# Weighted sum of gathered expert rows: from scalar-tensor steps on VectorE to diagonal matmuls on TensorE, with a new order of all engines in the last stage

## The reference

```python
gathered = ye[e_flat, jnp.minimum(pos, CAP - 1)]
gathered = jnp.where(valid[:, None], gathered, 0.0) * topk_w.reshape(-1)[:, None]
routed = gathered.reshape(T, K, D).sum(axis=1).reshape(B, S, D)
...
scores = jnp.einsum('bsd,bmd->bsm', hidden_states, memory_tokens) * scale
scores = jnp.where(memory_mask[:, None, :], scores, neg_inf)
attn = jax.nn.softmax(scores, axis=-1)
readout = jnp.einsum('bsm,bmd->bsd', attn, memory_tokens)
```

## Time and profile before

| | us |
|---|---|
| median of 3 runs | 396.79 (394.83 to 396.96) |
| the profiled execution, its own time | 392.95 |
| its span (first to last instruction of the program) | 391.1 |
| busy in the span: PE / DVE / ACT / POOL | 291.7 / 289.8 / 222.2 / 183.9 |
| first gather of the last stage is issued at | 205.62 |
| last instruction on DVE starts at | 387.47 |

### The profile page before, as it was taken

One profiled execution on the slowest core, in us unless ns is written; L12 is line 12 of the kernel. 1 busy time (PEld: TensorE's weight loads), 2 busy tenths in 40 slices (PEclk: granted clock), 3 DMA queues, 4 the chain that ended last, 5 costly groups with the idle time before them and its releaser, 6 DMA issues. The chain is left out here.

```text
span 391.1 us, 6082 instructions
## 1 busy us (share of the span) xinstructions
PE 291.7 (75%) x1748; PEld 221.5 (57%) x1748; DVE 289.8 (74%) x916; ACT 222.2 (57%) x394; POOL 183.9 (47%) x310
## 2 busy tenths in 40 slices
PE   1699899789999988966999055775757577576755
PEld 1488788667788866855988033343434334253433
DVE  1782359999989892854850656779999999999971
ACT  1112345444654455533635136566889797999883
POOL 3430133343342116777307777878786866323000
PEclk9999999999999999999999655575596988999898
DMA  7999200000008107689635232221211222000011
GB/s 193 363 422 426 99 28 28 28 28 28 28 0 338 40 6 223 154 137 158 215 134 188 81 100 63 80 69 42 80 45 63 77 69 71 3 28 28 14 41 56
DMA packets 22802, 41.80 MB, mean 107 GB/s; under 512 B 3631, under 2 KB 18417, under 8 KB 22129
## 3 DMA queue, kind: packets, MB, share of 16 engines
q1 hardware_dynamic: 15920, 26.72, 18.6%
q0 software_dynamic: 4672, 12.59, 13.8%
q10 hardware_dynamic: 2176, 2.10, 1.7%
HBM read 33.01 MB, written 8.39 MB: 106 GB/s over the span
## 5 line engine op out<-in xcount | busy, mean ns | idle before, releaser
L545 POOL DMA_INDIRECT big<-ye_dram,dst_all x64 | 69.0, 1079 | 35.9 <-issue 19.5
L751 PE MATMUL psum<-q_w,rh 128*128 128x512 bf16 x128 | 40.9, 457 | 11.9 <-DVE upT L1345 7.3
L1284 DVE SCALAR_TENSOR_TENSOR x_all<-big,wk_all,x_all 128x256 f32<-128x256 f32 x64 | 31.0, 484 | 19.7 <-DMA big<-ye_dram,dst_all 18.0
L526 POOL DMA_INDIRECT big<-xn_dram,tix x32 | 32.3, 1009 | 13.8 <-issue 7.5
L479 POOL TENSOR_SCALAR ve<-mv 128x2 f32<-128x2 f32 x16 | 7.8, 489 | 53.3 <-DVE mv L1046 43.3
L751 PE MATMUL psum<-ctx_all,shup 128*128 128x256 f32 x128 | 29.5, 383 | 0.0
L751 PEld LDWEIGHTS psum<-q_w,rh 128*128 128x128 bf16 x128 | 13.0, 112 | 28.2 <-issue 19.1
L572 ACT ACTIVATE xnT<-psum 128x512 f32<-128x512 f32 x24 | 14.3, 596 | 24.1 <-PE psum L899 21.2
L751 PEld LDWEIGHTS psum<-ctx_all,shup 128*128 128x128 f32 x128 | 23.7, 190 | 3.0
L572 ACT ACTIVATE big<-psum 128x512 f32<-128x512 f32 x16 | 9.5, 596 | 27.5 <-PE psum L775 17.8
L942 PE MATMUL psum<-ident,xn 128*128 128x128 f32 x32 | 7.1, 360 | 23.0 <-ACT xn L597 23.0
(11 more groups left out here) (198 smaller groups left out, 831.8 us busy)
## 6 DMA issues: line engine op xcount, KB each, us to landing
upT<-in_upT_dram SPq DMA_DIRECT2D x1, 4096.0 KB, 16.5
dnT<-in_dnT_dram SPq DMA_DIRECT2D x1, 4096.0 KB, 26.0
ye_dram<-rh SPq DMA_DIRECT2D x16, 256.0 KB, 3.0
ctxT_all<-in_ctxT_dram ACTq DMA_DIRECT2D x8, 256.0 KB, 8.7
x_all<-in_x_dram SPq DMA_DIRECT2D x8, 256.0 KB, 9.0
xn_dram<-xn SPq DMA_DIRECT2D x8, 256.0 KB, 2.1
out_dram<-x_all SPq DMA_DIRECT2D x8, 256.0 KB, 2.2
ctx_all<-in_ctx_dram SPq DMA_DIRECT2D x1, 1536.0 KB, 7.7
```

What stands on the lines that cost most here:

```text
L526: pl.indirect_dma_start(out=xe[:, q, e, :], out_offset=None, in_=xn_dram[:, :], in_offset=bass.IndirectOffsetOnAxis(ap=tix[:, 2 * i.c + e: ...
L545: pl.indirect_dma_start(out=gath[:, s, t * TOPK + k, :], out_offset=None, in_=ye_dram[:, :], in_offset=bass.IndirectOffsetOnAxis(ap=dst_al ...
L751: return pe.matmul(o, l, r, start=first, stop=last, skip_group_check=True)
L1284: c(dve.scalar_tensor_tensor(xt(i, t), gath[:, s, t * TOPK + k, :], w, xt(i, t), ALU.mult, ALU.add))
```

## The change

The four multiply-adds per tile on DVE are replaced. DVE now builds, per tile, four 128 x 128 matrices with the weights on the diagonal (`weight_diag`, one tensor-tensor of 128 x 512 values, into the free half of `big`). PE multiplies them with the four gathered tiles and adds up in bank 5 (`rows_sum`, four matmuls of 128 x 256 in float32). DVE adds the sum to x (`combine`, one instruction) and takes the statistics (`row_stats`). Bank 5 is shared with the scores, so `rows_sum` also waits for `exps`, and `score` for `combine`. The softmax scale of 1/16 goes into the mask constants and into `copy_x2T`, and the negated maximum comes from the reduction itself, so one small instruction of `smax` is dropped. The lists of all four engines are in another order and with other lags.

```diff
+        diag = big[:, 1, 0:4 * TOPK * P].rearrange("p (s t k m) -> p s t k m", s=2, t=2, k=TOPK)
...
-            pl.memset(mscale[:, :], -NEG)
-            pl.memset(mneg1[:, :], NEG)
+            pl.memset(mscale[:, :], -NEG * SM_SCALE)
+            pl.memset(mneg1[:, :], NEG * SM_SCALE)
...
                 def stage(i, s):
-                    hold(pl, (c4[t], 6 * (i.c - 2) + 4))
+                    hold(pl, (cmb[t], i.c - 1))
                     for k in range(2 * part, 2 * part + 2):
                         pl.indirect_dma_start(
...
-                (1, rows(0, 1)), (2, x2_rstd), (1, rows(1, 0)),
-                (3, rstd_shift(x34, lambda i: i.at(8, 8), mvx, vex, rsx, shx, LN_EPS, rs5)), (5, h_rstd),
-                (1, rows(1, 1)), (0, rows(0, 0))])
+                (2, x2_rstd), (3, rstd_shift(x34, lambda i: i.at(8, 8), mvx, vex, rsx, shx, LN_EPS, rs5)),
+                (1, rows(1, 1)), (5, h_rstd), (1, rows(1, 0)), (0, rows(0, 1)), (0, rows(0, 0))])
...
-                copy_to(xnT[:, s, :, :], bank(4, K, 2 * P), xT4)
+                copy_to(xnT[:, s, :, :], bank(4, K, 2 * P), xT4, scale=SM_SCALE)
...
+            def rows_sum(t):
+
+                def stage(i, s):
+                    before = (c4[0], 3 * i.c + 1) if t else (c4[1], 3 * i.c - 2)
+                    hold(pe, (gin[s][t], 16 * TOPK * (i.c // 2 + 1)), (dgs[t], i.c + 1), (ex4, i.c if t else i.c - 1), before)
+                    for k in range(TOPK):
+                        ins = mm_(bank(5)[:, 0:D], diag[:, s, t, k, :], gath[:, s, t * TOPK + k, :],
+                                  k == 0, k == TOPK - 1)
+                    ins.then_inc(cmb[t], 1)
+                return stage
...
-                hold(pe, (xT4, i.c + 1), (ex4, i.c))
+                hold(pe, (xT4, i.c + 1), (ex4, i.c), (c4[0], 3 * min(i.c + 1, NP - 1) + 1), (c4[1], 3 * i.c + 1))
...
+            def weight_diag(t):
+
+                def stage(i, s):
+                    hold(dve, (cmb[t], i.c - 1), (rb, RB * NP), (wqs, 3 * NG))
+                    dve.tensor_tensor(diag[:, s, t, :, :], ident[:, None, :].to_broadcast([P, TOPK, P]),
+                                      wk_all[:, 2 * i.c + t, :, None].to_broadcast([P, TOPK, P]), ALU.mult)\
+                       .then_inc(dgs[t], 1)
+                return stage
+
             def combine(t):
 
                 def stage(i, s):
-                    c = Chain(c4[t], i, 6)
-                    hold(dve, (gin[s][t], 16 * TOPK * (i.c // 2 + 1)))
-                    for k in range(TOPK):
...
+                    hold(dve, (cmb[t], i.c + 1))
+                    dve.tensor_tensor(xt(i, t), bank(5)[:, 0:D], xt(i, t), ALU.add).then_inc(c4[t], 1)
+                return stage
+
+            def row_stats(t):
+
+                def stage(i, s):
+                    hold(dve, (c4[t], 3 * i.c + 1))
+                    dve.bn_stats(bn[:, s, t, :], xt(i, t)).then_inc(c4[t], 1)
+                    hold(dve, (c4[t], 3 * i.c + 2))
+                    dve.bn_aggr(mv[:, s, t, :], bn[:, s, t, :]).then_inc(c4[t], 1)
                 return stage
...
-                dve.tensor_reduce(smx[:, s, :], bank(5)[:, 0:2 * P].rearrange("p (t m) -> p t m", t=2), AX.X, ALU.max)\
-                   .then_inc(mx4, 1)
-                hold(dve, (mx4, i.at(2, 1)))
-                dve.tensor_scalar(nmx[:, s, :], smx[:, s, :], -SM_SCALE, None, ALU.mult).then_inc(mx4, 1)
+                dve.tensor_reduce(nmx[:, s, :], bank(5)[:, 0:2 * P].rearrange("p (t m) -> p t m", t=2), AX.X, ALU.max,
+                                  negate=True).then_inc(mx4, 1)
...
-                (0, late_shared), (2, x3), (4, h_(1)), (4, hw_(1)), (0, combine(0)), (3, h_(0)), (6, final(1)), (1, smax), (4, hscale),
-                (5, final(0)), (2, x3_absmax), (2, x_scale), (2, x3_quant), (0, combine(1)), (3, hw_(0))])
+                (6, hscale), (0, weight_diag(0)), (2, row_stats(0)), (7, final(0)), (5, h_(1)), (5, hw_(0)),
+                (2, combine(1)), (2, row_stats(1)), (3, x3), (0, weight_diag(1)), (4, h_(0)), (1, combine(0)),
+                (5, hw_(1)), (3, x3_absmax), (3, x_scale), (2, smax), (3, x3_quant), (7, final(1)), (1, late_shared)])
```

More of the change, by code:

```diff
@@ L315, in build @@
         c4 = [sem(f"combined{t}") for t in range(2)]
+        dgs, cmb = [sem(f"weight_diag{t}") for t in range(2)], [sem(f"rows_summed{t}") for t in range(2)]
         rs4, xn4 = sem("x2_rstd"), sem("x2_normed")
@@ L957, in pt @@
             def pt(i, s):
-                hold(pe, (ex4, i.c + 1), (xT4, i.c + 1))
+                hold(pe, (ex4, i.c + 1), (xT4, i.c + 1), (qT5, i.c))
                 for t in range(2):
@@ L1015, in _ @@
             run_steps(pe, NP, [
-                (4, hqt(0)), (3, project(1, 1, (hd[0], 1))), (2, project(0, 0, (sl[1], 0))), (4, hqt(1)), (0, x2t),
-                (2, project(1, 0, (hd[1], 0))), (5, down(1, (sl[0], 4))), (4, hqt(2)), (0, score),
-                (4, down(0, (sl[0], 3))), (4, hqt(3)), (0, pt),
-                (2, project(0, 1, (sl[0], 1), (fo[0], -1), (fo[1], -2))), (0, read), (1, xqt)])
+                (1, rows_sum(1)), (2, read), (5, hqt(0)), (3, project(1, 0, (hd[1], 0))),
+                (3, project(0, 1, (sl[0], 1))), (0, rows_sum(0)), (1, x2t), (5, hqt(1)),
+                (3, project(1, 1, (hd[0], 1))), (1, score), (6, down(1, (sl[1], 4))), (5, hqt(2)),
+                (5, down(0, (sl[1], 3))), (2, xqt), (5, hqt(3)), (1, pt),
+                (2, project(0, 0, (sl[1], 0), (fo[0], -2), (fo[1], -3)))])
         @block.vector
```

31 lines of the change are left out of this document (10 added, 21 removed).

## The result

In the timing the changed kernel has a median of 392.8 us over 20 runs, the kernel before 394.84 us over 20. The ratio is 0.994 with a 95% interval of [0.9914, 0.9966]: 0.6% faster, where 1.0% was forecast. The profiled execution took 391.8 us, its span is 390.1 us with a granted clock of 0.949, 1.0 us less than the span of before.

The account below looks back on a forecast made before the run. VectorE bounds the steady turn, busy 17.61 of 18.4 us. Turns -4.4, ramp +4.0, drain -3.7 sum to -4.1 us, so 396.79 becomes 392.7 us, 1.0% faster; range 386 to 402.

Parts of the forecast that it names:

- Prices of instructions: Durations per instruction: diagonal product 0.68 us, addition from PSUM 0.48, row sum of four matmuls 1.8 high clock, 3.6 low.
- Steady turn: Items 3 to 7: VectorE 16.5, GpSimd 16.7, ScalarE 16.0 us; turn 18.0 to 16.9, four turns -4.4 us (-6.4 to 0).
- signs of being wrong: In the changed profile: steady row sums of 3.6 us, GpSimd waiting over 1 us for VectorE there, or a free ramp.
- The row sum closes a loop: Rival, steady turns: lap through `pt`, gate projection and row sum, 16.2 us high clock, 19.1 low; about 404 us; chance 0.18.
- Ramp: Up to item 3's `x2_rstd`: row sums on TensorE delay it, +5.6 us low clock, +2.4 high; +4.0 taken (0 to +5.6).
- Drain: From item 7's `x2_rstd` to the end: -3.7 us (-3.7 to -2.5), of which -2.5 from `hw_(0)` no longer before `smax`.
- further -1.2: Rest of the drain: -1.2 us for the smaller sum in `smax` and better packing of `hquant` and `down`; 0 as other end.
- The shared port: GpSimd and two-SBUF-input VectorE instructions exclude each other; GpSimd's 16.7 us may fall by 0.8, the sum by at most 0.2 a turn.

Follow-up runs that it names:

- the staggered run: Changed kernel with GpSimd issuing all eight gathers in the item's own turn, six tile-1 gathers of items 1 and 2 one turn later; 388.64 us, 0.9864 to before.
- run 6: Changed kernel plus unused bf16 matmuls filling TensorE's waits for items 0 to 4; six executions from 389.47 to 404.04 us, no ratio given.
- the order only: Kernel before with the new lists of all engines and smaller softmax step, but old four multiply-adds, no diagonals or row sums; 390.78 us, ratio 0.9851.

## Why the prediction was right, and where it was not

**The total.** 392.7 us was forecast, 392.8 measured. The agreement in us is partly luck, since the kernel before has a median of 394.84 in the timing, not 396.79; in per cent it is 1.0 against 0.6, and from span to span -1.0 us against -4.1.

**Prices of instructions: right.** Diagonal product 0.69 us (0.68 forecast), addition 0.42 (0.48), row sum 1.99 at the 2.4 GHz level and up to 3.78 at 1.2 (1.8 and 3.6).

**Steady turn: mechanism partly wrong, term mis-sized.** The step that failed is "I take 16.9", from VectorE's 16.5 and GpSimd's 16.7. The loads fell as forecast: VectorE is busy 15.55 and 15.19 us a turn, GpSimd 13.38 and 13.00 beside its issues. The turn was 17.4 all the same, as the engines wait in a loop that no sum of one engine's work contains: -2.3 us over four turns, not -4.4. The text had said that the gathers now stand behind a late `x3` with TensorE's list behind them, and gave that no price. Taking them away from there is worth 1.5 us a turn (17.4 to 15.9), and then GpSimd's queue, put at 16.7 us, is full in turns of 16.5 and 16.7. Two of the signs of being wrong that the prediction named struck: GpSimd waited over 1 us for VectorE in two of the turns (1.61 at 285.72, 1.18 at 303.87), and in the same two turns the tile-1 sum took 3.78 and 3.54 us, the low level. The clock's share, about 3.3 us by those rows, would cover the 2.1 us between the 67.6 forecast for four turns and the 69.7 measured. But the gathers' loop is there without it: in the other two turns TensorE, at the high level, waits 1.73 and 1.09 us for rows, and the staggered run came to 63.5 us with two slow sums of its own.

**The row sum closes a loop: right as a mechanism, for the wrong first loop.** The rival's lap through `pt` and the gate projection was put at 16.2 us at the high level. In the changed kernel it is hidden by the gathers' loop by the 0.95 to 1.73 us that TensorE waits for rows. With the gathers early it comes out at 16.3 us (284.47 to the end of the statistics at 300.78), close to the 16.2, with part of the sum at the low level. But GpSimd's queue ends within 0.1 us of it, so that run doesn't say that this lap sets the turn.

**Ramp: size right, reason open.** +4.0 was taken, +3.2 measured; items 2 and 3 came at 252.24 and 267.51, within the forecast, item 1 at 235.74, earlier than 238. But the working made it TensorE's clock, +5.6 low and +2.4 high, and run 6 gives 45.9 us with the clock high, 46.2 without, with added work in the chain that hides what the clock gives back. What the traces do show is that GpSimd, which had no gap there in the earlier trace rows, now waits 1.88, 1.72 and 0.49 us for statistics, 4.1 of the 4.3 us by which this ramp is longer than that of the order only (41.9): the sums have tied `x2_rstd` to the attention chain and to landings. How much of these waits is the clock (sums of 3.78 and 2.39 us) and how much the place of the sums, no run separates. The warning of the Trainium skill (TensorE: Matmul & The Clock Gate, section "Why this matters for your kernels") that idle gaps drop the clock fits the level of 0.89 and 0.74 in the ramp and the sum of 3.54 us at 299.00; what it cost in time is open for the ramp. The order alone takes 1.1 us off the ramp (43.0 to 41.9), so the sums cost 4.3 there.

**Drain: half right.** From item 7's `x2_rstd` to its maximum it is 6.7 us (337.25 to 343.92) after 9.7, so -3.0 where -2.5 was worked out. The further -1.2 was a guess and came out as +1.1: 42.6 us remain to the end, before 41.4. Why was not tested.

**The order as such.** The sum had no term for it beside the drain. The run with the order only says -1.5% (-1.1% by its medians), the smaller softmax step included. Its profiled execution shows +0.8 up to item 0's `x2_rstd`, -1.1 in the ramp, -1.8 in the turns and +0.6 in the drain, -1.5 us in all; the first statistics step, 1.04 us in the earlier trace rows, takes 0.24 there. That the forecast still hit means that two errors met: VectorE's relief was worth less than assumed, the order more. Between the profiles of the changed kernel and the order-only one the last VectorE instruction differs by 0.5 us, between the ratios it is 0.9%; the profiles thus explain only part of that difference, and only 1.5 us of the 4.5 to 5.9 that the order gains by medians and ratio.

**The shared port.** The rule of the Trainium skill, SBUF — State Buffer, section "SBUF: two separate sides", was given little weight, at most 0.2 us a turn. `ve` takes 0.22 to 0.24 us in all items of the changed kernel but the first (0.51), where it took 1.02 to 1.05 from item 4 on. But `ve` is 0.24 with the old multiply-adds in the new order too, so it was the new order with its other neighbours that did that, not the removal of the multiply-adds. The rule itself holds again on the next step: `vex` takes 0.61 us at 306.01, beside the diagonal product of 305.85 to 306.54 with its two SBUF inputs, and 0.22 one turn later (323.09), with no such product beside it. The same shows on the gather behind it, which the prediction didn't look at: in the four turns it takes 1.83 to 1.93 us, begins 0.3 to 0.4 us after the product of `hw_(0)` and ends 1.0 us after that product does (308.38 and 310.22, the product from 307.99 to 309.21). In the ramp, behind `x2_rstd` of items 1 and 2, with no such product beside it, it takes 1.15 and 1.14 us. That is 0.7 us of each lap of the gathers' loop, and 0.4 more come from `vex`; so GpSimd is held up here now, and no longer at `x2_rstd`. No run moved the product to test it.
